# A latent-attention block between two feed-forward layers: P x V stored unjoined and unscaled, joined in the output stage

## What is computed

```
q = _rmsnorm(x @ wq_a.T, q_a_ln_w) @ wq_b.T              # 32 heads of 64 + 64
ckv, k_pe = split(x @ wkv_a.T)                           # 64 latent values, 64 rotary
kv = _rmsnorm(ckv, kv_a_ln_w) @ wkv_b.T                  # per head 64 of k, 128 of v
scores = einsum('bqhd,bkhd->bhqk', q_full, k_full) * softmax_scale   # causal
out = einsum('bhqk,bkhd->bqhd', softmax(scores), v).reshape(B, S, H * VD)
return out @ wo.T
```

## Time and profile before

| | us |
|---|---|
| median of 3 runs (lowest, highest) | 1893.46 (1892.46, 1895.08) |
| profiled execution, its own time and its span | 1895.1, 1895.1 |
| TensorE busy | 1803.7 (95%) |
| VectorE busy | 1231.4 (65%) |
| ScalarE busy | 1000.5 (53%) |
| GpSimd busy | 877.8 (46%) |

### The profile page before, as it was taken

How to read it: one execution, slowest core, us unless ns; L and a number is a source line. 1 busy time by engine, 2 the same in 40 slices (tenths; PEclk the granted TensorE clock), 3 DMA queues, 4 the chain that set the end, 5 groups by cost and what they waited for, 6 DMA issues and landing times. The chain is left out here.

```text
span 1895.1 us, 44298 instructions
## 1 busy us (share of the span) xinstructions
PE 1803.7 (95%) x15472; PEld 1422.9 (75%) x15472; DVE 1231.4 (65%) x2654; ACT 1000.5 (53%) x2137; POOL 877.8 (46%) x641
## 2 busy tenths in 40 slices
PE   5999969899999999999999999998999999989999
PEld 4788869877777777777777777775788888877887
DVE  5655358688898888889888888989521111125453
ACT  2221047788887888888787888877310100112110
POOL 3232112377777878777787878775000000014321
PEclk9999979999999999999999999999999999989999
DMA  6542162311212112121222212123742233224321
GB/s 217 193 156 100 67 173 94 84 62 44 86 59 78 57 62 80 57 80 40 85 69 68 69 51 82 55 86 113 249 151 89 94 100 115 67 87 158 130 89 59
DMA packets 111969, 182.74 MB, mean 96 GB/s; under 512 B 27680, under 2 KB 64672, under 8 KB 109856
## 3 DMA queue, kind: packets, MB, share of 16 engines
q1 hardware_dynamic: 111904, 181.88, 29.8%
HBM read 122.33 MB, written 59.51 MB: 96 GB/s over the span
## 5 line engine op out<-in xcount | busy, mean ns | idle before, releaser
L1290 PE MATMUL psS<-keyT,q 128*128 128x512 f32 (+2 forms) x2304 | 473.2, 350 | 23.9 <-POOL q L648 14.5
L1290 PEld LDWEIGHTS psS<-keyT,q 128*128 128x128 f32 x2304 | 381.2, 189 | 118.2 <-DVE negmax L1408 41.7
L1357 ACT ACTIVATE prob<-prob,negmax 128x640 f32<-128x640 f32 (+7 forms) x512 | 392.0, 767 | 78.5 <-DVE negmax L1408 75.9
L1418 DVE STREAM_TRANSPOSE pT<-prob 128x640 f32<-128x640 f32 (+7 forms) x512 | 379.9, 762 | 66.4 <-PE psV L1307 61.6
L1408 DVE CUSTOM_DVE_ANT_0 prob<-psS,mask 128x640 f32<-128x640 f32 (+7 forms) x512 | 371.9, 742 | 20.9 <-PE psS L1290 7.4
L469 PE MATMUL f_psy<-f_weff,f_xT 128*128 128x512 f32 x1344 | 315.6, 393 | 0.0
L1101 PE MATMUL psS<-o_w,o_o 128*128 128x512 f32 x1344 | 304.8, 389 | 0.0
L469 PEld LDWEIGHTS f_psy<-f_weff,f_xT 128*128 128x128 f32 x1344 | 250.9, 188 | 55.8
L1101 PEld LDWEIGHTS psS<-o_w,o_o 128*128 128x128 f32 x1344 | 252.3, 188 | 52.4
L1307 PE MATMUL psV<-pT,val 32*64 32x512 f32 (+3 forms) x8192 | 264.8, 407 | 6.4 <-DVE pT L1418 6.2
L1307 PEld LDWEIGHTS psV<-pT,val 32*64 32x64 f32 x8192 | 168.8, 132 | 109.7 <-issue 66.2
(11 more groups left out here) (120 smaller groups left out, 1919.1 us busy)
## 6 DMA issues: line engine op xcount, KB each, us to landing
wo<-in_wo SPq DMA_DIRECT2D x16, 1024.0 KB, 6.0
pT<-row_scales SPq DMA_DIRECT2D x128, 128.0 KB, 2.9
oT<-pT SPq DMA_DIRECT2D x64, 256.0 KB, 2.5
o_in<-oT SPq DMA_DIRECT2D x32, 512.0 KB, 5.2
f_xt<-in_x SPq DMA_DIRECT2D x16, 512.0 KB, 4.4
f_w_in<-in_w SPq DMA_DIRECT2D x16, 512.0 KB, 6.7
w_sum<-f_w_in SPq DMA_DIRECT2D x16, 512.0 KB, 5.3
x<-f_xo SPq DMA_DIRECT2D x16, 512.0 KB, 3.0
```

The source lines that it names most:

```text
L1290: ins = nc.tensor.matmul(psS[:, slot, start + x0:start + x1], q[:, e, a, t * P:(t + 1) * P], k.keyT[:, m, b * S + x0:b * S + x1], start=(i ...
L1357: nc.scalar.activation(row, row, ACT.Exp, bias=negmax[:, n % 8:n % 8 + 1], scale=-1.0, accum_out=rowsum[:, column(n, s):column(n, s) + 1]) ...
L1418: nc.vector.transpose(pT[:, n % 2, t, 0:width], prob[:, n % RING, 0:width]).then_inc(turned, 1)
```

## The change

V's two halves are no longer joined or scaled in the loop. ScalarE copies each bank of `psV` whole, 128 x 512, into `o_raw`, now twice as large; VectorE's job O, GpSimd's job P and the broadcast load of the scales are gone. SP stores the four pieces of `o_raw` to `o_parts` and the turned scales to `row_scales`, both laid out so that a row of a token tile runs over pairs first. In the output stage SP loads per half tile six pieces: even parts into `o_in`, odd parts and broadcast scales into the not yet used low and high halves of the tile `o`; GpSimd adds and then multiplies (`join_outputs`), 128 x 1024 each. Tile 1 now runs after tile 0, and later tiles close both halves of the result together. All four order tables that had these jobs are new in their order too. The core of the diff:

```diff
@@ order tables
...
-POOL_STEP = ("B2+0 B3+0 A0+1 A1+1 B0+1 B1+1 P0-1 P1-1 A2+1 A3+1")
+POOL_STEP = ("B2+0 B3+0 A0+1 A1+1 B0+1 B1+1 A2+1 A3+1")
@@ class Output
-        self.o_in = at("o_in", "wo", 0, [P, PAIRS, P])
+        self.o_in = at("o_in", "cosT", 0, [P, PAIRS, P])
...
-        self.x_in = [at("o_x_in0", "cosT", 0, [P, D]), at("o_x_in1", "sinT", 0, [P, D])]
+        self.x_in = [at("o_x_in0", "wo", 0, [P, D]), at("o_x_in1", "wo", row, [P, D])]
...
-    def load_outputs(self, sp, n):
+    def load_outputs(self, sp, n, j, h):
+        x = slice(h * PAIRS * P // 2, (h + 1) * PAIRS * P // 2)
+        parts = self.parts_d.rearrange("(n e h v) m -> e h v n m", n=NT, e=2, h=2)[:, :, :, bass.ds(n, 1), x]
+        for e in range(2):
+            rows = slice(KVR * e, KVR * e + KVR)
+            even, odd = (parts[e, i].rearrange("v a m -> v (a m)") for i in range(2))
+            scale = self.scales_v[e, bass.ds(n, 1), x].to_broadcast([KVR, PAIRS * P // 2])
+            sp.dma_start(self.o_in[rows, self.half_of(h), :].rearrange("p a n -> p (a n)"), even).then_inc(self.o_loaded[h], 16)
+            sp.dma_start(self.raw(j, LO, h)[rows, :], odd).then_inc(self.o_loaded[h], 16)
+            sp.dma_start(self.raw(j, HI, h)[rows, :], scale).then_inc(self.o_loaded[h], 16)
+
+    def join_outputs(self, nc, pool, n, j):
         for h in range(2):
-            sp.dma_start(self.o_in[:, self.half_of(h), :], self.oT_v[:, self.half_of(h), bass.ds(n * P, P)]).then_inc(self.o_loaded[h], 16)
+            both = self.o_in[:, self.half_of(h), :].rearrange("p a n -> p (a n)")
+            pool.wait_ge(self.o_loaded[h], n * 96 + 96)
+            nc.gpsimd.tensor_tensor(both, both, self.raw(j, LO, h), ALU.add).then_inc(self.o_joined, 1)
+            pool.wait_ge(self.o_joined, n * 2 + h + 1)
+            nc.gpsimd.tensor_tensor(both, both, self.raw(j, HI, h), ALU.mult).then_inc(self.o_scaled, 1)
...
@@ sync_steps
                 sp.wait_ge(self.o_lo, n * 2 + 2)
-                self.load_outputs(sp, n + 1)
+                sp.wait_ge(self.product, n * 2)
+                for h in range(2):
+                    self.load_outputs(sp, n + 1, (j + 1) % 2, h)
@@ outputs_hi
-        act.wait_ge(self.o_loaded[h], n * 16 + 16)
+        act.wait_ge(self.o_scaled, n * 2 + h + 1)
@@ weights_hi, and alike weights_lo
-            if pair in (0, 1, 8, 9):
-                self.outputs_hi(nc, act, pair // 8, pair // 8, pair % 2)
+            if pair in (5, 7):
+                self.outputs_hi(nc, act, 0, 0, pair // 7)
@@ tensor_steps
+        for pair in range(PAIRS):
+            pe.wait_ge(self.o_lo, 2 * pair // PAIRS + 1)
+            pe.wait_ge(self.w_lo, pair + 1)
+            add_pair(0, pair, pair == PAIRS - 1)
+        for pair in range(PAIRS):
+            pe.wait_ge(self.o_lo, 2 * pair // PAIRS + 3)
+            add_pair(1, pair, pair == PAIRS - 1)
...
@@ store_o on SP
-            def store_o(it, ch, s):
+            def store_o(it, e, s):
                 b, pair = s % 2, it + s // 2
-                sp.wait_ge(scaled, (it * 2 + s) * 2 + ch + 1)
-                sp.dma_start(oT_d[bass.ds(pair * P, P), b * S + ch * CHUNK:b * S + (ch + 1) * CHUNK], o_raw[:, ch, :]).then_inc(o_stored[ch], 16)
+                sp.wait_ge(evicted, (it * 2 + s) * 4 + 4)
+                parts = parts_d.rearrange("(n e p) m -> e p n m", n=NT, e=2)[e, :, :, bass.ds(pair * P, P)]
+                for a in range(2):
+                    n = b * QT + a * QT // 2
+                    sp.dma_start(parts[:, n:n + QT // 2, :],
+                                 o_raw[:, 2 * e + a, :].rearrange("p (t q) -> p t q", q=P)).then_inc(o_stored, 16)
@@ SP, last round and after it
-                        sp.wait_ge(w_done, units)
-                        sp.wait_ge(o_stored[0], 16 * (units - 1))
-                        output.load_outputs(sp, 0)
+                        sp.wait_ge(queries.roped, 4 * units)
+                        for ch in range(2):
+                            sp.wait_ge(r_stored[ch], 64 * PAIRS)
+                        sp.wait_ge(o_stored, 64 * (units - 1))
+                        for h in range(2):
+                            output.load_outputs(sp, 0, 0, h)
...
+            output.load_weights(sp, range(3 * SLOTS, 14))
+            sp.wait_ge(output.o_lo, 2)
+            output.load_outputs(sp, 1, 1, 0)
+            output.load_weights(sp, range(14, PAIRS))
+            output.load_outputs(sp, 1, 1, 1)
@@ evict_values on ScalarE
                 if later(step, 1):
-                    act.wait_ge(evicted, step * 4 + bank - 3)
-                nc.scalar.activation(upper(bank), psV[KVR:P, bank, :], ACT.Copy).then_inc(copied, 1)
+                    act.wait_ge(o_stored, step * 64)
+                nc.scalar.activation(by_block(o_raw, bank), psV[:, bank, :].rearrange("p (a t r) -> p a t r", a=4, r=32),
+                                     ACT.Copy).then_inc(evicted, 1)
@@ VectorE
-            def join_values(it, bank, s):
...
@@ GpSimd
-            def scale_values(it, ch, s):
...
             rounds(pool, body)
+            output.pool_steps(nc, pool)
```

More of the change, by code:

```diff
@@ L1057, in vector_steps @@
     def vector_steps(self, nc, dve):
+        for h in range(2):
+            self.outputs_lo(nc, dve, 1, 1, h)
         def step(n, j, has):
@@ L1077, in tensor_steps, with add_pair @@
     def tensor_steps(self, nc, pe):
[L1078 to L1091 removed]
+        def add_pair(j, pair, closing):
+            for half in range(2):
+                x = slice(half * BANK, (half + 1) * BANK)
+                for i, (a, m) in enumerate(PASSES):
+                    ins = nc.tensor.matmul(self.ps[:, j, x], self.o[j][:, a, pair, :], self.w[pair][:, m, x],
+                                           start=(pair == 0 and i == 0), stop=(pair == PAIRS - 1 and i == 2))
+                if closing:
+                    ins.then_inc(self.product, 1)
@@ L1226, in body @@
                     if job == "X":
[L1227 removed]
+                        store_scales(r.it, n, s)
                     elif job == "Y":
@@ L1394, in _ @@
             output.weights_hi(nc, act, range(2 * SLOTS, 14))
-            for ch in range(2):
-                act.wait_ge(o_stored[ch], 16 * units)
+            act.wait_ge(o_stored, 64 * units)
             output.weights_hi(nc, act, range(14, PAIRS))
@@ L1429, in row_scales @@
                 if later(number, 4):
[L1430 removed]
+                    dve.wait_ge(r_stored[x // QT], (it + s // 2) * 64)
                 nc.vector.transpose(rinvT[:, x // QT, :], rinv[:]).then_inc(r_turned, 1)
[L1433 to L1444 removed]
             nc.vector.memset(rinv[:], 1.0).then_inc(zeroed, 1)
@@ L1456, in body @@
                         row_scales(r.it, n, s)
-                    elif job == "O":
-                        if r.last and s == 1 and n == 0:
-                            output.weights_lo(nc, dve, range(2 * SLOTS))
-                        join_values(r.it, n, s)
                     elif job == "F":
@@ L1463, in _ @@
             rounds(dve, body)
-            output.weights_lo(nc, dve, range(2 * SLOTS, PAIRS))
+            output.weights_lo(nc, dve, range(PAIRS))
             output.vector_steps(nc, dve)
```

136 lines of the change are left out of this document (48 added, 88 removed).

## The result

| | before | changed |
|---|---|---|
| median (lowest, highest), us | 1893.05 (1892.46, 1895.08), 4 runs | 1915.47 (1912.91, 1918.99), 4 runs |
| profiled span, us | 1895.1 | 1913.1 |
| TensorE, VectorE, ScalarE, GpSimd busy, us | 1803.7, 1231.4, 1000.5, 877.8 | 1800.7, 1152.6, 1007.6, 947.2 |

The ratio to before is 1.0117, 95% interval 1.0102 to 1.0131: 1.2% slower, clear of the noise. I had forecast 1854, with a range to 1880.

What follows compares the result with a forecast made beforehand. TensorE was taken to bound loop and output stage, with VectorE holding it back in the loop. Loop -41, last unit -3, output tiles 0 and stage start +4 sum to -40: 1854 us against the median, range 1838 to 1880.

Steps and rivals of the forecast that it cites:

- Output tiles 2 to 15: Output stage: 14 tiles stay at 21.8 us each, loads and joins hidden behind TensorE's tile; change 0.
- 3 MB at 304 GB/s: Output stage: the twelve loads of a tile take 10 us, first half landing at about 7, second at 12.
- Rival 3: Output tiles: loads of 64 partitions bound them, 35 us a tile, +182 us, 2031 us in all; chance 0.07.
- My 19 us: Output tile: 3 MB at 196 and 1 MB at 328 GB/s take 19 us, still under 21.8.
- Start of the output stage: Tiles 0 and 1 with the weights, after the last V: +4 us, ends -6 and +20.
- rival 2: Start of the output stage costs 20 us, not 4; time 1870 us; chance 0.13.
- VectorE's slowing: Start of the output stage: eight GpSimd operations each add 1.1 us to a VectorE subtraction, 9 us.
- Loop: Attention loop: a unit falls from 30.28 to 28.9 us, over 30 intervals -41 us, ends -56 and -8.
- 25.7 us, 2.7 under TensorE's floor: Loop, VectorE per unit: 23.3 us of work plus about 2.4 us waiting for V's first part before T0.
- TensorE's floor: Loop, TensorE per unit without waits: 27.8 us without folds, 29.0 with two, mean 28.4.
- Last unit: Loop's last unit, with no next one to fill TensorE: -3 us.
- Rival 1: Loop: ScalarE or GpSimd takes VectorE's place at about 29.7 us a unit; 1877 us; chance 0.17.

Runs made afterwards that it cites:

- Experiment 1: Changed kernel with SP loading each half tile once that half of the tile before is split, steps written out; 1876.05 us, ratio 0.9904.
- experiments 2 and 5: Changed kernel with 128-partition loads, wrong rows: six of 512 KB a tile (1867.98 us), or twelve of 256 KB with half the columns (1867.24 us).
- experiment 8: Kernel with half-tile waits, wide part loads and weights first; tile 1's scales loaded for one pair only, wrong output; 1869.60 us.
- experiment 3: Changed kernel without GpSimd's multiplication by the scales, all loads kept, wrong output; 1876.64 us.
- experiments 1 to 8: Eight follow-up runs that edit waits, loads, scales, joins or weight order around the output stage of the changed kernel; single times from 1867.24 to 1917.32 us.
- experiment 14: Kernel with half-tile waits, wide part loads, weights first and early reciprocal; S10 put ahead of Q0 in TensorE's table; 1910.37 us, ratio 1.0092.

## Why the prediction was wrong

- **Output tiles 2 to 15: predicted 0, measured +36.** This is the step that failed. Its sentence "The load for tile n+1 may start when tile n-1 is done" is false: the diff keeps `sp.wait_ge(self.o_lo, n * 2 + 2)` above the wait for the product, and `o_in` exists once. The load starts when both halves of tile n are split. I summed 20 us for loads, joins and splits and compared them with a deadline one tile away; they had to be compared with a period, since they run in a ring. With my own numbers the ring closes in 20 us, under 21.8, so the second error was needed too: 3 MB at 304 GB/s. The loads took 16.7 us to the second half's landing, not 12. Experiment 1 removes the first error's cause, experiments 2 and 5 the second's, and either alone brings back 21.8 us.
- **Rival 3 was the right side and nearly the right mechanism**, "decides ... when twelve loads take over 25 us". They didn't; loads of 17 us were enough, because 7 us of joins and splits stand in series with them. I gave it 0.07 on a price (35 us) that was too high and a threshold that was too high as well. The windows show the slow side of it: 241 GB/s at full share with loads of 64 partitions, 328 with 128. The Trainium skill, "SBUF — State Buffer", "Door 1", which I had set aside, has 196 GB/s for 64 partitions against 328, and the trace agrees in direction; a quarter of the bytes in the window of 241 are wide. An estimate from its figure: the 3 MB in the ring at 196 GB/s are 16 us, and with the 7.2 us of joins and splits 23, over TensorE's 21.8. The trace has 16.67 and 24.04. My 19 us counted the tile in and out, which aren't in the ring, and was compared with the tile with nothing added.
- **Start of the output stage: +4 (ends -6, +20), measured +18.6.** Inside the ends, at the upper one; rival 2's 20 us. The half wait was 3.7 of it, narrow part loads 1.8, the order of the weights 0.3. What is left, 12.8 us, isn't divided by any run: experiment 8 shows 2.55 us for 0.9 of the 4 MB more, so volume is in it, and experiment 3, 8.4 us sooner with every byte loaded, shows that the joins and their use of the engines are in the 18.6 too. VectorE's slowing, which I had priced at 9 us, measured 25.0 us for 16 weight subtractions against 21.3 before, 3.7 more; what that costs the stage isn't shown.
- **Loop: V to V 28.9, measured 29.17**, 32.8 us of the 41. VectorE lost 2.6 us of busy time per unit, not 3.3 (52.85 to 47.67 in two units), its idle time before T0 is 2.47 as said, ScalarE's copies took 600 ns as said. Failed was "25.7 us, 2.7 under TensorE's floor": T0 is not the only place where VectorE waits for V. M8 needs S8, which is behind all of V, so VectorE idles another 1.14 us there (or 1.57). And TensorE's floor was too low: the unit without folds has no idle row left and still takes 28.41 us, not 27.8. S14 and S15, which I had priced at 2.72 us, take more: S12 to S14 stand from 838.71 to 843.05, 4.34 us, of which S12 and S13 had needed 2.53 before (796.74 to 799.27), and S15 takes 1.51. S0 to S7 take 3.96, not 3.83. Whether this is their own price or a wait too short to be listed isn't shown, nor is what closes the unit.
- **Last unit: -3, measured -1.7** (27.64 to 25.92 from V to V). **Start of the loop:** the first V came 1.0 us earlier, which can't be told from the spread: over experiments 1 to 8, whose loops have the same order, it came from 384.5 to 386.7, and in the kernel before at 386.6.
- Rival 1's size, 29.7, didn't come; its thought, that ScalarE is close behind, is borne out by experiment 14.

## What to carry to other kernels

Where a stage has one input buffer, add up load, join and split as a ring and compare that sum with the period of the engine it feeds, not with a deadline a tile ahead; look for the latest wait of the loading queue, also where the diff leaves it untouched. A rate from a window holds for transfers of that width: see how many partitions each load covers before it is used. And where an order written by hand has little idle time left on any chain, single moves in it may do harm more often than good (2 of 5 here did nothing, 3 cost 6 to 39 us).
